# Wavelet attention: queries' and keys' rows spread on GpSimd in groups of four heads, and turned by DMA transposes instead of TensorE

## The reference

```python
xe, xo = x[:, 0::2], x[:, 1::2]
a, det = (xe + xo) * inv, (xe - xo) * inv        # 1024 positions of 128 channels
q, k, v = (a @ wq), (a @ wk), (a @ wv)           # each (B, 1024, 16 heads, 8)
att = softmax(einsum("bqhd,bkhd->bhqk", q, k) / sqrt(8))
o = einsum("bhqk,bkhd->bqhd", att, v).reshape(B, 1024, D) @ wo
y = interleave((o + det) * inv, (o - det) * inv)
return _same_dwconv(y, conv_w)                   # 4 taps along the tokens
```

## Time and profile before

| | |
|---|---|
| median of 3 runs | 4496.69 us (4492.57 to 4499.21) |
| profiled execution | 4491.74 us, its span 4490.4 us |
| mean granted clock | 0.822 |
| PE / DVE / ACT / POOL busy | 80% / 75% / 65% / 21% |
| wavelet attention | about 570 to 1164 us of the span, both ends included |

### The profile page before, as it was taken

The page is one execution under the profiler, slowest core; times in us unless marked ns, Lnnn a source line. Parts: engine busy times, 40 slices in busy tenths (PEclk is TensorE's granted clock), DMA queues, the critical chain, the costliest instruction groups (busy, mean ns, idle before and its releaser), DMA issues.

```text
span 4490.4 us, 75098 instructions
## 1 busy us (share of the span) xinstructions
PE 3603.3 (80%) x29334; PEld 1878.8 (42%) x29334; DVE 3359.9 (75%) x5235; ACT 2904.4 (65%) x4864; POOL 921.4 (21%) x1314
## 2 busy tenths in 40 slices
PE   6999869899599998899997555555555558899998
PEld 4666523232244445666665111111111114566666
DVE  6778687786420117777886999999999996778887
ACT  3665336656343435566664999999998995566665
POOL 2444401000166660000001232222132210000000
PEclk8999869999799999999998555555555558899999
DMA  1000000000321100000000111110111100000000
GB/s 47 1 1 1 1 3 1 1 1 1 84 53 38 38 7 18 9 9 11 2 2 15 22 22 22 21 20 18 19 22 21 22 19 20 6 11 6 8 2 21
DMA packets 155438, 72.36 MB, mean 16 GB/s; under 512 B 122419, under 2 KB 140478, under 8 KB 155070
## 3 DMA queue, kind: packets, MB, share of 16 engines
q1 hardware_dynamic: 155086, 67.56, 7.0%
HBM read 31.75 MB, written 2.23 MB: 8 GB/s over the span
## 4 chain that ended last, share of the span: by engine, by line
PE 43%; DVE 27%; issue 14%; ACT 4%; DMA 1%; POOL 0%; SPq 0%; DVEq 0%; ACTq 0%; POOLq 0%
DVE d_negmax L2734 12%; PE psum L2265 6%; PE psum L2294 6%; DVE f_m_E L2364 6%; PE psum L2280 6%; PE psum L1925 5%; PE psum L1949 5%; PE psum L1307 3%; PE psum L1296 2%; DVE f_pT_E L2383 2%; DVE wl_negmax L1421 2%; PE psum L1275 2%; ACT d_junk L2792 2%; PE psum L2667 1%; ACT wl_p L1559 1%
## 5 line engine op out<-in xcount | busy, mean ns | idle before, releaser
L2734 DVE TENSOR_REDUCE d_negmax<-psum 128x1 f32<-128x1024 f32 x1024 | 1176.7, 1216 | 52.1 <-PE psum L2667 50.9
L2792 ACT ACTIVATE d_junk<-psum,d_negmax 128x1024 bf16<-128x1024 f32 x1024 | 1137.9, 1113 | 103.8 <-DVE d_negmax L2734 96.0
L2667 PE MATMUL psum<-d_qT,d_kT 64*128 64x512 bf16 x2048 | 605.7, 601 | 549.3 <-ACT d_junk L2792 529.6
L2458 ACT ACTIVATE hidden<-psum,f_nm_E 128x1024 f32<-128x1024 f32 x512 | 566.0, 1112 | 144.1 <-DVE f_nm_E L2367 144.0
L2364 DVE TENSOR_REDUCE f_m_E<-psum 128x1 f32<-128x1024 f32 x512 | 602.2, 1218 | 47.7 <-PE psum L2265 46.4
L2667 PEld LDWEIGHTS psum<-d_qT,d_kT 64*128 64x128 bf16 x2048 | 105.8, 101 | 1050.5 <-ACT d_junk L2792 990.2
L2265 PE MATMUL psum<-f_k_E,f_q_swapped_E 64*128 64x512 f32 x1024 | 527.4, 625 | 6.5 <-ACT hidden L2458 6.5
L2265 PE MATMUL psum<-f_k_E,f_q_E 64*128 64x512 f32 x1024 | 527.0, 625 | 3.1 <-DMA f_q_swapped_E<-f_q_E 1.1
L2465 ACT COPY f_pT_E<-psum 128x512 f32<-128x512 f32 x512 | 299.4, 585 | 322.8 <-PE psum L2280 322.8
L2294 PE MATMUL psum<-f_pT_E,f_v_E 128*64 128x128 f32 x8192 | 505.4, 276 | 2.5 <-DVE residual L2394 2.5
L2383 DVE COPY f_pT_E<-psum 128x512 f32<-128x512 f32 x512 | 351.8, 687 | 160.5 <-PE psum L2280 150.6
(11 more groups left out here) (337 smaller groups left out, 4664.7 us busy)
## 6 DMA issues: line engine op xcount, KB each, us to landing
moe_gates_on_all<-moe_gate_spill SPq DMA_DIRECT2D x16, 1024.0 KB, 13.7
f_q_swapped_E<-f_q_E SPq DMA_DIRECT2D x64, 128.0 KB, 2.3
moe_w<-in_moe_w SPq DMA_DIRECT2D x16, 256.0 KB, 5.7
out<-residual SPq DMA_DIRECT2D x1, 2048.0 KB, 8.7
residual<-in_hidden_states SPq DMA_DIRECT2D x2, 768.0 KB, 7.8
residual<-in_hidden_states SPq DMA_DIRECT2D x2, 256.0 KB, 3.2
m_taps<-in_m_conv SPq DMA_DIRECT2D x4, 128.0 KB
level_sums<-in_c_sums SPq DMA_DIRECT2D x1, 512.0 KB
```

Source lines behind the costliest of these rows:

```text
L2458: A.activation(pb[:, u % 2, f * 2 * BANK:(f + 1) * 2 * BANK], two(2 * f), ACT.Exp, bias=nm[:, u % 4:u % 4 + 1], scale=SC, accum_out=rs[:, ...
L2667: last = T.matmul(bank(2 + 2 * (at % 3) + jj), kT[half, s, jb * P:(jb + 1) * P], qT[half, s, hf * BANK:(hf + 1) * BANK], start=True, stop= ...
L2734: V.tensor_reduce(mh[:, t % 2, n // 2, n % 2:n % 2 + 1], two(2 + 2 * (at % 3)), X, ALU.max, negate=True).then_inc(*maxed.up(at))
L2792: A.activation(junk[:, at % 3, :], two(2 + 2 * (at % 3)), ACT.Exp, bias=mh[:, t % 2, n // 2, n % 2:n % 2 + 1], accum_out=sh[:, t % 2, n // ...
```

## The change

Rows are no longer spread for a whole sequence, but for one round (four heads) at a time, and nearly all by POOL: nine copies for k and nine for q of 128 x 256 elements, where there were three shared by three engines of 128 x 512. DVE makes only the first q. `wl_q_rows` has two buffers of four heads, `wl_k_rows` one, and a head's columns are padded to 128.

All turning is done by DMA transposes issued by SP, one for two heads (16 blocks of 128 x 128). `sp_rows` issues four (q, k, q, k), `sp_shifted` two. TensorE, ACT and DVE have no part in it any more, and nothing of it takes a PSUM slot.

The order changes too. Four `exp` steps open a round. From the fourth on one `max` follows each, and two follow every third, so that the last `max` comes after the 27th `exp`. The next round's `shift` stands there, five `exp` ahead of the round's end. The parts of sequence 1 are made by POOL at the beginning of (0,2). `wl_diff` and `wl_v` get a second buffer of their own, where the second half lay in `residual`. The expert stage after it no longer loads the tokens (`residual`, 2 MB) again.

```diff
-                uq = sb(st, "wl_q_rows", [P, CT, NH, PITCH], BF16)
-                uk = sb(st, "wl_k_rows", [P, CT, NH, PITCH], BF16)
-                qT = sb(st, "wl_qT", [ROWS, 8, B2], BF16)
+                uq = sb(st, "wl_q_rows", [P, 2, 4, CT, P], BF16)
+                uk = sb(st, "wl_k_rows", [P, 4, CT, P], BF16)
+                qT = sb(st, "wl_qT", [P, 8, B2], BF16)
...
                 for n, (b, g) in enumerate(rounds_c):
-                    seq.append(("shift", b, g))
                     if n:
                         seq.append(("fin", *rounds_c[n - 1]))
-                    seq += [("qrow", b, h) for h in range(4 * g, 4 * g + 4)]
-                    ahead = maxes(*rounds_c[n + 1]) if n + 1 < len(rounds_c) else []
-                    first_ahead = 9 if (b, g) == (0, HB - 1) else 0
+                    ahead = []
+                    if n + 1 < len(rounds_c):
+                        seq.append(("rows", *rounds_c[n + 1]))
+                        ahead = maxes(*rounds_c[n + 1])
                     for u in range(4 * CT):
-                        if u >= first_ahead and ahead:
-                            seq += ahead.pop(0)
                         seq.append(("exp", b, g, u // 4, u % 4))
+                        for _ in range((1 + (u % 3 == 2)) if u >= 3 else 0):
+                            if ahead:
+                                seq.append(ahead.pop(0))
+                                if not ahead:
+                                    seq.append(("shift", *rounds_c[n + 1]))
+                        if u == 2 and n + 2 < len(rounds_c) and (b, g) != (0, 2):
+                            seq.append(("spread", *rounds_c[n + 2]))
...
+                def sp_rows(b, g):
+                    n = round_at[b, g]
+                    SP.wait_ge(*spread_q(b, g))
+                    SP.wait_ge(*spread_k(b, g))
+                    if n >= 2:
+                        SP.wait_ge(*second_pass(*rounds_c[n - 2], CT - 1, 3))
+                    for hh in (0, 2):
+                        SP.dma_start_transpose(in_lanes(qT, 4 * g + hh), in_blocks(uq[:, n % 2, hh:hh + 2])).then_inc(*turned["q_turned"][hh // 2].one())
+                        SP.dma_start_transpose(in_lanes(kT, 4 * g + hh), in_blocks(uk[:, hh:hh + 2])).then_inc(*turned["k_turned"][hh // 2].one())
+
+                def sp_shifted(b, g):
+                    SP.wait_ge(*max_rows(b, g))
+                    n = round_at[b, g]
+                    if n:
+                        SP.wait_ge(*second_pass(*rounds_c[n - 1], 0, 3))
+                    if n and n + 1 < len(rounds_c):
+                        SP.wait_ge(*spread_q(*rounds_c[n + 1]))
+                    for hh in (0, 2):
+                        SP.dma_start_transpose(in_lanes(qT, 4 * g + hh), in_blocks(uq[:, round_at[b, g] % 2, hh:hh + 2])).then_inc(*turned["q_shifted"][hh // 2].one())
...
                 def pe_max(b, h, i):
                     if i == 0:
-                        T.wait_ge(*rows_q(b, h))
-                        T.wait_ge(*rows_k(b, h))
+                        T.wait_ge(*q_rows(b, h))
+                        T.wait_ge(*k_rows(b, h))
...
+                def spread(e, step, w, b, g):
+
+                    n = round_at[b, g]
+                    for half in range(2):
+                        e.wait_ge(*parted(b, half, 2))
+                    if w == "q" and n >= 2:
+                        for hh in range(4):
+                            e.wait_ge(*q_again(rounds_c[n - 2][0], 4 * rounds_c[n - 2][1] + hh))
+                        step(e.memset(uq[:, n % 2, :, :, MR:MR + 3], 0.0))
+                    if w == "k" and n:
+                        for hh in range(4):
+                            e.wait_ge(*k_rows(rounds_c[n - 1][0], 4 * rounds_c[n - 1][1] + hh))
...
+                    for i in range(3):
...
+                        for j in range(3):
+                            last = e.tensor_copy(u[:, :, :, i, j, :] if w == "q" else u[:, :, :, j, i, :], src)
                     return last
```

More of the change, by code:

```diff
@@ L1159, in phase_C @@
                         seq += extra.get((b, g), {}).get(u, [])
-                    for item in ahead:
-                        seq += item
+                        if u == 2 and (b, g) == (0, 2):
+                            seq.append(("spread", *rounds_c[n + 2]))
                 seq += [("fin", *rounds_c[-1]), ("norm", *rounds_c[-1])]
                 seq += [("co", 1), ("wo", 1)] + [("conv", 1, c) for c in range(4)] + [("yt", 1, 0), ("yt", 1, 1)]
-                paired = [s for s in seq if s[0] in ("turn", "qkv", "rows", "max", "qrow", "exp", "norm", "co", "wo", "yt")]
+                paired = [s for s in seq if s[0] in ("turn", "qkv", "max", "exp", "norm", "co", "wo", "yt")]
                 slot_of = {s: n % 3 for n, s in enumerate(paired)}
@@ L1215, in sp @@
                             SP.dma_start(gain[:, n:n + 1], a[t][2, :].rearrange("(p o) -> p o", o=1)).then_inc(*ld.one())
+                    for kind, *u in seq:
+                        if kind == "rows":
+                            sp_rows(*u)
+                        elif kind == "shift":
+                            sp_shifted(*u)
                     leave(SP)
@@ L1295, in pe_exp @@
                     for j in range(2):
-                        last = T.matmul(bank(bk + j), kT[:, h, kt * P:(kt + 1) * P], qT[:, h, j * BANK:(j + 1) * BANK], start=True, stop=True)
+                        last = T.matmul(bank(bk + j), kT[0:ROWS, h, kt * P:(kt + 1) * P], qT[0:ROWS, h, j * BANK:(j + 1) * BANK], start=True, stop=True)
                     last.then_inc(*second_pass.up(b, g, kt, hh))
```

168 lines of the change are left out of this document (52 added, 116 removed).

## The result

| | before | after |
|---|---|---|
| median of 16 runs each | 4496.38 us (4483.19 to 4504.64) | 4509.64 us (4502.68 to 4517.17) |
| profiled execution, span | 4491.74, 4490.4 | 4517.17, 4515.9 |
| mean granted clock | 0.822 | 0.811 |

The ratio is 1.0035, with an interval of 1.0026 to 1.0045: the change costs 12 to 20 us. The forecast was 4498; the measured median lies between it and the rival of 4518, at the upper edge of the span that the prediction gave its own case (4486 to 4510). The two profiled executions stand 25.4 us apart, more than the medians (13.3), since the one of after is the longest of its runs and the one of before lies under its median. Rounds read from them are therefore a few us too far apart in all.

What follows compares the result with a forecast made beforehand. Bound: the ring of three PSUM slots with TensorE in order. Start, round and boundary terms total +4.0 us on the profiled 4491.7, giving 4495.7; forecast 4498, between profiled and median scales, own case 4486 to 4510, full range 4464 to 4526.

Steps and rivals of the forecast that it cites:

- the rival of 4518: Clock, once fallen in the boundary gap, stays down 13.5 us a round; +20 us on the forecast; chance 0.23.
- Start: Before the first round: parts sooner, POOL copies and two transposes added, k-row copies gone; net +0.6 us, bounds -4 and +6.
- The boundary: Between rounds: queued transposes land 2.6 us apart, so the first maximum starts 13.8 us after the shift begins.
- the cases of 4469 and 4534: Queued transposes land 2.0 us apart (-29 us, chance 0.23) or 4.3 apart (+36 us, chance 0.08).
- The middle: From a round's first maximum: two stretches of maxima and exponentials in the new order end after 44.1 us; bounds 36.5 and 47.
- The rule of three slots: In the PSUM ring, a unit starts when TensorE is free and the unit three before is consumed; old order 6.25 us.
- The failed term is the clock: TensorE's clock falls in each round's boundary gap for 6 us, costing 2.3 us.
- rate of 0.38: In the stage's rounds, a spell of x us at 1.2 GHz costs 0.38x.
- a plain round: A round without extra work, 58.5 us before, becomes 61.9: +3.4 us.
- POOL was not hidden: POOL's 18 copies a round, 7 to 11 us, were called hidden within 40 us, also beside part-making in (0,2).
- (0,3) and (1,0): (0,3) loses late spreads and lone maxima, -10.5 us; (1,0) has DVE work fall in its gap, -1.6 us.
- The rest of the span: Outside the rounds: the token reload removed from the expert stage lay beside a busy TensorE, worth nothing.

Runs made afterwards that it cites:

- experiment 8: Kernel before, with two maxima ahead of every second exponential instead of one ahead of each; 4547.20 us, ratio 1.0123.
- experiment 4: Kernel before, turning still on TensorE, with only the changed kernel's order of maxima and exponentials; 4529.68 us, ratio 1.0088.
- experiment 3: Changed kernel with a third buffer of turned rows, a round's transposes issued one round earlier, token reload back; 4484.73 us, ratio 0.9992.
- experiment 1: Changed kernel with one more wait: POOL makes the parts of sequence 1 only after the shift of (0,2); 4498.70 us, ratio 1.0024.
- Experiment 11: Changed kernel with wl_diff and wl_v back in residual and the token reload back, still two buffers; 4516.58 us, ratio 1.0051.
- experiment 6: Changed kernel with a third buffer of turned rows, POOL's parts after the shift of (0,2), and the old order; 4490.78 us, ratio 0.9997.
- experiments 5: Changed kernel, two buffers and all turning by DMA, with the order of the kernel before; 4533.25 us, ratio 1.0089.

## Why the prediction was right, and where it was not

The answer lies inside the range, on the side with the largest chance (slower, 0.41; the terms add up to 0.42). But the likeliest case's number, 4498, was 12 us too low: by that number there would have been no change to measure. That the total came so near is partly luck, since two misses of 8 us in the first three rounds cancel. The steps:

- **Start**: +0.6 predicted, +0.2 measured. POOL's k copies in the kernel after, by their tile (ns min/median/max), stand near the lower of the two bounds, 0.395 to 0.63:

```profile
L1385 POOL COPY wl_k_rows<-wl_parts x72: 399/406/417, 596.7 to 1010.3; 128x256 bf16<-128x256 bf16 x72
```

- **The boundary was right.** The first M is at S+13.5 (13.8). Queued transposes land about 2.5 apart ((13.5 - 1.65 - 4.3) / 3, 2.6 taken), which rules out 2.0 and 4.3 apart, and so the cases of 4469 and 4534. The windows have 207 to 220 GB/s at a share of 1.13 to 1.15. The Trainium skill ("DMA: Bandwidth & Descriptors", "Latency and other measured facts") has 261 GB/s for a transpose whose middle dimension is not contiguous; the trace stays under it. By the price of one block in the Trainium skill ("VectorE: DVE Perf Modes", "The three transpose paths") 16 blocks would take 20.9 us, an estimate; here 16 take 2.5 when they are queued.
- **The middle was right at the full clock, as far as can be seen.** The rule of three slots gave 6.25 for the even order as in the trace; for pairs it gave 6.9 in the expectation of experiment 8, and 6.94 was measured. No whole middle of the changed order ran at the full clock, so the 44.1 itself was not seen. What the prediction did not do is to price the order by itself: it took the middle of 44.1 as part of one change, and never said that this order costs the kernel before 39 us (experiment 4).
- **The failed term is the clock.** One spell of 6 us a round was taken, 2.3 us. There were three falls in the round that was read, with 17 us at 1.2 GHz, 14.5 of them in the middle, and the middle took 51.7 instead of 48.1. The prediction's own rate of 0.38 would make 5.5 of 14.5, so 3.2 of the 3.6 that are over (an estimate). Its price for a us at the low clock was sound; the length was not. The +3.4 of a plain round was +7.6 (15.3 / 2). Seven rounds of 3.6 more would be 25; the sum of the stage was 17.6 over the forecast in these two executions (+21.6 against +4.0), since (0,0) and (0,1) did better: 132.6 in all, where 135.5 was the time before. By the stage's clock the change has 88 us more at 1.2 GHz than before, 33 us by the same rate, where seven spells of 6 make 16: the 17 between them are the whole excess, to some 4 us. The rival of 4518 was a little nearer in number, and its 13.5 us at the low clock in each round are nearer to the 17 than the 6. But it had them as one spell after the gap. The later two falls come in stretches without a gap, and in experiment 3, where the gap is gone, all three stay. So the reason that both gave for the first fall, the gap, is not borne out.
- **POOL was not hidden.** "24 to 28 us in all still fit" counted POOL's own time, and it was there. What failed was the tacit step that DVE runs freely beside it: the issue came 5.6 us late in (0,2), and experiment 1 took 5.5 off that round. The first three rounds' total (203.6 for 202.8) hides this: (0,2) alone was +10.8, where +2.4 was forecast.
- **(0,3) and (1,0)** gave 6.6 back where 10.5 was expected, and +2.0 where it was -1.6. Each is about the 3.6 of the middle. For (1,0) experiment 1 shows that it hangs on the clock: 73.1 at 0.81, and 67.7 at 0.91 with the same work.
- **The rest of the span** was 3.9 longer in this pair of executions. Later stages have no changed work but the missing reload, which was put at nothing. Experiment 11 puts it at 7 us in the change's favour, with an interval that does not leave out nothing; the 3.9 are a loss all the same, and what they are is open.

What stays open: why the clock falls in some nearly busy stretches and not in others. Two things went with a lower clock. One is a less even order (0.94 before, 0.91 with the order alone, 0.89 with pairs). The other is the work taken from TensorE: 0.91 to 0.85 from experiment 4 to the kernel after, with the order kept, and 1.00 to 0.91 in (1,2) from the kernel before to experiment 6, where the orders are nearly the same. By the rate of 0.38 the step from 0.91 to 0.85 is 21 us (an estimate), so the clock may have taken back as much as was left of the gain. But no run changed the clock alone; the nearest are the two rounds (1,0) of experiment 1. The split of the 39 us of experiment 4 between slots and clock is therefore an estimate, and only its sum is shown.

## What to carry to other kernels

A change can be a gain and a loss in one: here the moved work gave 24 us and the order that came with it cost 39. Work out the price of a new order by itself, on the old kernel, before joining it to the change that asked for it. Where the transfers that a step waits for stand behind others in the queue, give them a buffer so that they can go earlier: that was worth 4 us a round with the changed order and 9 with the even one (67.4 to 58.2 in (1,2), experiments 5 and 6). Once they are in time, hiding them further brought nothing in a plain round. And read the clock of single rounds: two rounds with the same instructions can differ by 5 us through it.

## What the runs showed of the hardware

- Small DVE instructions that began beside a POOL instruction on float32 ended with it: a cast of 128x32 from float32 to bf16 took 2.22 us beside a POOL subtraction of 2.13, and 0.25 without it. A subtraction of 128x32 took 1.05 beside POOL's cast of 1.04, and 0.21 without it. The Trainium skill ("SBUF — State Buffer", "SBUF: two separate sides") has a port pair that one of the two holds for a whole instruction, for DVE instructions in a two-port mode, or of two SBUF inputs against a GpSimd one that reads SBUF. The trace agrees for the subtraction, which has two inputs in SBUF; it shows the same for the cast, but not in which mode that ran.
- A DMA transpose of 16 blocks took SP 1.9 us to issue when it was alone. With others before it in the queue the medians of the three lines were 2.16, 2.22 and 2.85 (L1224, L1213, L1214), up to 3.63, and it landed 4.7, 4.9 and 5.0 after its issue instead of 4.3. Queued, they landed 2.5 apart.
- The granted clock fell to 0.50 in stretches in which TensorE was busy for 1.51 and 1.82 of 2.00 us, and not only across a gap; at the boundary it fell with the idle gap of 3.95 us and, in experiment 3, without it.
